# Attention softmax by two sets of scores, one turned, with the maximum added on TensorE, in a step per batch

## The reference, cut to what matters

```python
x = x + L0_xattn(layernorm(x), ctx, ctx, ...)   # rotary embedding on q and k
x = x + L0_ffn(layernorm(x), ...)               # 8 experts, top 2, and a shared one
x = x + L1_xattn(layernorm(x), ctx, mask, ...)  # no rotary; keys masked where mask is 0
x = x + L1_ffn(layernorm(x), ...)               # 16 experts, top 4, and shared ones

# one attention, for each batch and each of 16 heads
q = (query @ Wq.T + bq);  k = (key @ Wk.T + bk);  v = (key @ Wv.T + bv)
scores = einsum('bhsd,bhtd->bhst', q, k) / sqrt(16)      # 128 queries x 128 keys
attn = softmax(scores, axis=-1)
out = einsum('bhst,bhtd->bhsd', attn, v)                 # then @ Wo.T + bo
```

## Time and profile before

| what | value |
|---|---|
| three timed runs | 1117.19, 1118.29, 1121.87 us |
| the profiled execution: its own time | 1119.13 us |
| its span, first to last instruction | 1117.3 us |
| TensorE matmul busy / weight load busy | 952.8 us (85%) / 825.7 us (74%) |
| VectorE / ScalarE / GpSimd busy | 776.6 / 581.0 / 436.6 us |
| mean granted TensorE clock | 0.940 of full |

### The profile page before, as it was taken

How to read it: one execution, slowest core, us unless ns; L and a number is a source line. 1 busy time by engine, 2 the same in 40 slices (tenths; PEclk the granted TensorE clock), 3 DMA queues, 4 the chain that set the end, 5 groups by cost and what they waited for, 6 DMA issues and landing times.

```text
span 1117.3 us, 20415 instructions
## 1 busy us (share of the span) xinstructions
PE 952.8 (85%) x6981; PEld 825.7 (74%) x6981; DVE 776.6 (70%) x1538; ACT 581.0 (52%) x1112; POOL 436.6 (39%) x479
## 2 busy tenths in 40 slices
PE   2798878748987999999837888885989999999995
PEld 2577667536877999999825767665678888888885
DVE  5688787866664777777655687795686666667665
ACT  5375675745234667667546877874622232322221
POOL 1465556240663666666415444334012212212210
PEclk9989999859998999999956899996899999999999
DMA  3300750010325888888540000001000001000002
GB/s 129 110 21 1 189 144 1 1 61 1 128 82 193 237 231 233 227 221 233 119 134 1 20 20 1 1 2 43 15 15 29 28 14 28 17 26 28 14 0 76
DMA packets 44281, 85.81 MB, mean 77 GB/s; under 512 B 4161, under 2 KB 31041, under 8 KB 44097
## 3 DMA queue, kind: packets, MB, share of 16 engines
q0 software_dynamic: 14784, 46.44, 15.1%
q1 hardware_dynamic: 29440, 38.61, 11.9%
HBM read 64.25 MB, written 20.79 MB: 76 GB/s over the span
## 4 chain that ended last, share of the span: by engine, by line
PE 48%; DVE 20%; ACT 11%; issue 9%; DMA 7%; POOL 4%; DVEq 0%; ACTq 0%; POOLq 0%
PE bank L1179 31%; PE bank L1215 8%; DMA w_raw<-in_fw,w_idx 4%; DVE nmax L1034 3%; PE bank L1274 3%; DVE probT_lo L1063 2%; PE bank L1364 2%; DVE prob L1037 2%; POOL sorted_x L375 2%; ACT xn L512 2%; DMA summed<-y_sb,tile_to 2%; ACT probT_hi L654 1%; ACT o_raw L644 1%; PE bank L1343 1%; ACT w_hi L533 1%
## 5 line engine op out<-in xcount | busy, mean ns | idle before, releaser
L1179 PE MATMUL bank<-xT_hi,w_hi 128*128 128x512 f32 x352 | 139.9, 398 | 2.2 <-DVE hid L964 2.2
L581 ACT ACTIVATE act_sb<-bank 128x512 f32<-128x512 f32 x88 | 52.6, 598 | 167.8 <-PE bank L1179 167.7
L1179 PE MATMUL bank<-xT_lo,w_hi 128*128 128x512 f32 x352 | 139.3, 396 | 0.0
L1179 PE MATMUL bank<-xT_hi,w_lo 128*128 128x512 f32 x352 | 139.1, 395 | 0.0
L964 DVE TENSOR_TENSOR hid<-bank,act_sb 128x512 f32<-128x512 f32 x88 | 60.8, 691 | 107.3 <-ACT act_sb L581 107.1
L332 POOL TENSOR_TENSOR w_hi<-w_raw,zero_col 128x768 fp32r<-128x768 f32 (+1 forms) x20 | 31.9, 1595 | 262.9 <-PE bank L1215 236.8
L951 DVE SCALAR_TENSOR_TENSOR xres<-bank,gate,xres 128x256 f32<-128x256 f32 x320 | 132.6, 476 | 0.8 <-PE bank L1215 0.8
L1364 PE MATMUL bank<-ident,prob 128*128 128x128 f32 x512 | 86.2, 298 | 31.9 <-DVE probT_lo L1063 26.0
L1063 DVE TENSOR_TENSOR probT_lo<-bank,probT_hi 128x512 f16<-128x512 f32 x128 | 88.0, 687 | 32.4 <-ACT probT_hi L654 31.8
L1179 PE MATMUL bank<-xsT_hi,w_hi 128*128 128x256 f32 x368 | 106.5, 289 | 2.3 <-DVE xsT_lo L918 1.5
L1215 PE MATMUL bank<-w_hi,hid_hi 128*128 128x256 f32 x352 | 99.5, 283 | 6.2 <-DVE hid_lo L972 6.2
(11 more groups left out here) (199 smaller groups left out, 2763.5 us busy)
## 6 DMA issues: line engine op xcount, KB each, us to landing
w_raw<-in_fw SPq DMA_DIRECT2D x18, 384.0 KB, 3.0
sorted_x<-empty_row SPq DMA_DIRECT2D x2, 2967.0 KB, 21.4
xs<-sorted_x SPq DMA_DIRECT2D x23, 258.0 KB, 3.4
ctx_raw<-in_ctxT SPq DMA_DIRECT2D x8, 512.0 KB, 5.2
aw_raw<-in_aw SPq DMA_DIRECT2D x10, 256.0 KB, 3.8
summed<-empty_row SPq DMA_DIRECT2D x1, 2304.0 KB, 29.6
xres<-in_x SPq DMA_DIRECT2D x4, 512.0 KB, 5.7
xn_all<-summed SPq DMA_DIRECT2D x4, 512.0 KB, 5.9
```

The lines of the kernel that those rows point to most:

```text
L581: nc.scalar.activation(act_sb[:, (ls * J + j) % 2, :], bank[2 * ((ls * J + j) % 2) + 1][:], ACT.Silu).then_inc(f["act"], 1)
L1179: last = nc.tensor.matmul(dst, lh, rh, start=(i == 0), stop=(i == len(pairs) - 1))
```

## The change

Each batch becomes one step, and every engine's program is written out over 16 batches and two steps of tail. Scores are made twice. `scores` makes them queries by keys, only for the maximum: banks 0 to 3, all four row groups, the zeroed copy now being of Q (`q_half`), 128 columns to a product. VectorE's four reductions of a batch write the negated maxima to columns of `low_col`; TensorE turns that tile (`lows_turned`), ScalarE copies it (`low_copy`) to `low_row`. `scores_turned` makes the scores keys by queries in banks 4 to 7 and adds the negated maximum there by products with `pick`, a 0/1 tile that has a one in the row of the head. ScalarE's exponential of a whole bank then gives the probabilities with keys on partitions, so nothing is turned or split: `weighed` multiplies them in float32 by `v_full` (16 columns of V, one of ones, padded to `VW` = 32) with V as the weights, into four 32-partition strips of bank 0. ScalarE copies this, TensorE turns it back (`turned_back`), VectorE normalizes (`output`). The layer 1 mask is a bias of the exponential by key (`mask_col`, one more DMA) and a product in `scores`. Outputs are projected batch by batch.

Layer 0 no longer has the exchanged weights (four weights in place of six): VectorE multiplies one product by cosine and by sine and exchanges partitions in pairs by `stream_shuffle`, GpSimd subtracts. A step makes at most two items of a later block (`build_at`): steps 0 to 2 K0 and K1, Q0 and Q1, V0 and V1 of block 1; steps 3 to 5 and 7 to 9 K0 and V0, K1 and V1, Q0 and Q1 of blocks 2 and 3. GpSimd keeps the rotary subtraction, the context's low part and bias additions. `lowest` in a step waits for all of `scores`.

The diff, cut to its core:

```diff
-VW = 50
-RING, RINGT = 6, 3
+VW = 32
-        W_ORDER = [[2, 3, 0, 1, 4, 5], [1, 2, 0, 3]]
+        W_FROM = [[0, 2, 4, 5], [0, 1, 2, 3]]
+        W_ORDER = [[K_W, Q_W, V_W, O_W], [K_W, V_W, Q_W, O_W]]
@@ sync @@
+                sp.dma_start(mask_col[:], maskrow.rearrange("o (b t) -> (o t) b", t=S),
+                             allow_slow_non_contiguous=True).then_inc(s_in, 16)
@@ scalar @@
+                def attend():
+                    context_high(1)
+                    low_copy(0)
+                    for b in range(B + 2):
+                        if b < B:
+                            exponential(b, 0)
+                            exponential(b, 1)
+                        if 1 <= b <= B:
+                            output_copy(b - 1)
+                        if b < B:
+                            exponential(b, 2)
+                            exponential(b, 3)
+                        if b >= 2:
+                            output_high(b - 2)
...
+                        if b + 1 < B:
+                            low_copy(b + 1)
@@ vector @@
+                    dve.wait_ge(a["rope"], 3 * u + 2)
+                    nc.vector.stream_shuffle(rope_b[:, r], rope_b[:, r], PAIR).then_inc(a["rope"], 1)
...
+                def attend():
+                    lowest(0)
+                    for b in range(B + 2):
+                        if b + 1 < B:
+                            lowest(b + 1)
+                        if b >= 2:
+                            output_low(b - 2)
+                        made = build_at(b)
+                        if made:
+                            made_item(made[0], made[1])
+                        if 1 <= b <= B:
+                            output(b - 1)
+                        if b >= 2:
+                            residual(b - 2)
+                        if made:
+                            made_item(made[0], made[2])
@@ tensor @@
+                def scores(b):
...
+                    for u in range(KT):
+                        for h in range(2):
+                            for r in range(NG):
+                                rows = slice(32 * r, 32 * r + 32)
+                                at_col = 256 * u + S * h
+                                last = nc.tensor.matmul(bank[r][:, at_col:at_col + S], q_half[rows, n % 2, u, h, cols],
+                                                        k_full[rows, n % 2, u, cols], start=(u == 0 and h == 0),
+                                                        stop=(l == 0 and u == KT - 1 and h == 1))
...
+                def scores_turned(b):
+                    n, c = divmod(b, BLK)
+                    if b >= 1:
+                        pe.wait_ge(a["exp"], NG * b)
+                    if b >= 3:
+                        pe.wait_ge(a["xadd"], b - 2)
+                    made = build_at(b - 1) if b else None
+                    for item in made[1:] if made else ():
+                        banks_read(made[0], item)
+                    cols = slice(S * c, S * (c + 1))
+                    for u in range(KT):
+                        for r in range(NG):
+                            rows = slice(32 * r, 32 * r + 32)
+                            nc.tensor.matmul(bank[4 + r][:, 256 * u:256 * u + 256], k_full[rows, n % 2, u, cols],
+                                             q_half[rows, n % 2, u, :, cols], start=(u == 0), stop=False)
+                    pe.wait_ge(a["lowcopy"], b + 1)
+                    for h in range(GRP):
+                        for r in range(NG):
+                            rows = slice(32 * r, 32 * r + 32)
+                            last = nc.tensor.matmul(bank[4 + r][:, S * h:S * (h + 1)], pick[rows, h, :],
+                                                    low_row[rows, b % 2, :], start=False, stop=(h == GRP - 1))
+                    last.then_inc(a["turn"], 1)
...
+                def weighed(b):
+                    n, c = divmod(b, BLK)
+                    pe.wait_ge(a["exp"], NG * (b + 1))
...
+                    if b + 2 < B:
+                        pe.wait_ge(a["max"], NG * (b + 2) + 1)
+                    for pair in range(2):
+                        for u in range(KT):
+                            for q in range(4):
+                                r, j = 2 * pair + q // 2, q % 2
+                                last = nc.tensor.matmul(bank[0][32 * q:32 * q + VW, S * (2 * u + pair):S * (2 * u + pair + 1)],
+                                                        v_full[:, n % 2, c, 8 * u + 2 * r + j, :],
+                                                        prob[:, b % 2, r, S * (2 * u + j):S * (2 * u + j + 1)],
+                                                        start=True, stop=True)
...
+                def attend():
+                    scores(0)
+                    lows_turned(0)
+                    for b in range(B + 2):
+                        made = build_at(b)
+                        if b < B:
+                            scores_turned(b)
+                        if b + 1 < B:
+                            scores(b + 1)
+                        if 1 <= b <= B:
+                            weighed(b - 1)
+                        if b >= 2:
+                            output_turned(b - 2)
+                        if made:
+                            pe.wait_ge(a["exp"], NG * b + 1)
+                            make_item(made[0], made[1])
+                        if 1 <= b <= B:
+                            turned_back(b - 1)
+                        if b >= 2:
+                            projected(b - 2)
+                        if made:
+                            pe.wait_ge(a["exp"], NG * b + 2)
+                            make_item(made[0], made[2])
+                        if b + 1 < B:
+                            lows_turned(b + 1)
```

More of the change, by code:

```diff
@@ L475, in _ @@
-                outputs(NBLK - 1, False)
-                pool.wait_ge(a["xadd"], 2 * NBLK)
+                context_low(a, 1)
+                for b in range(B):
+                    made = build_at(b)
+                    for item in made[1:] if made and l == 0 else ():
+                        if item not in (V0, V1):
+                            rotate(made[0], item)
+                    if b in (2, 5):
+                        context_low(a, 2 + b // 4)
+                pool.wait_ge(a["xadd"], B)
@@ L587, in experts @@
                                              ACT.Copy).then_inc(f["hhi"], 1)
[L589 removed]
+            act.wait_ge(s_set, 2)
             for l in range(2):
@@ new lines, in values @@
+                def values(m, item):
+                    h = (V0, V1).index(item)
+                    if m == 0:
+                        dve.wait_ge(a["vset"], 2)
+                    dve.wait_ge(a["vps"], 2 * m + h + 1)
+                    src = bank[unit_bank(l, m, item)]
+                    for c in range(2):
+                        nc.vector.tensor_tensor(v_full[:, m % 2, 2 * h + c, :, 0:HD],
+                                                src[:, D * c:D * (c + 1)].rearrange("p (h d) -> p h d", h=HEADS),
+                                                bv_row[l][:].rearrange("p (h d) -> p h d", h=HEADS),
+                                                ALU.add).then_inc(a["v"], 1)
@@ L1101, in _ @@
-                    values(0)
+                    for item in (K0, K1):
+                        unit_build(0, item)
+                    weights_low(range(2, NW))
+                    for item in (Q0, Q1):
+                        unit_build(0, item)
+                    for item in (V0, V1):
+                        values(0, item)
                     first_constants()
@@ new lines, in unit, with wt @@
+                def unit(m, item):
+                    u = unit_no(m, item)
+                    w, r = (K_W, Q_W)[item in (Q0, Q1)], u % 2
+                    def wt(part):
+                        return lambda k: part[:, w, k, P * r:P * (r + 1)]
+                    if item in (K0, K1):
+                        pe.wait_ge(a["ctx_lo"], m + 1)
+                        right = (lambda k: ctx_hi[:, k, :], lambda k: ctx_lo[:, k, :])
+                    else:
+                        cols = slice(N * m, N * (m + 1))
+                        right = (lambda k: xT_hi[:, k, cols], lambda k: xT_lo[:, k, cols])
+                    products(bank[unit_bank(l, m, item)][:], (wt(aw_hi), wt(aw_lo)), right).then_inc(a["proj"], 1)
@@ new lines, in values @@
+                def values(m, item):
+                    pe.wait_ge(a["ctx_lo"], m + 1)
+                    h = (V0, V1).index(item)
+                    for c in range(2):
+                        rows = slice(P * (2 * h + c), P * (2 * h + c + 1))
+                        last = products(bank[unit_bank(l, m, item)][:, D * c:D * (c + 1)],
+                                        (lambda k: ctx_hi[:, k, rows], lambda k: ctx_lo[:, k, rows]),
+                                        (lambda k: aw_hi[:, V_W, k, :], lambda k: aw_lo[:, V_W, k, :]))
```

(1 more changed line is left out.)

678 lines of the change are left out of this document (290 added, 388 removed).

## The result

The changed kernel takes 1127.41 us (median of 11 runs, 1123.09 to 1135.96), the kernel before in the same session 1118.81 (11 runs, 1115.91 to 1125.31). The ratio is 1.0081, 95% interval 1.0052 to 1.0111: slower by 0.8%. Forecast were 1099 us and a gain.

The account below looks back on a forecast made before the run. The prediction took VectorE's throughput in the attentions as the bound. Gains of 20.1 us in layer 0 and 8.1 in layer 1, less 9.0 for the clock, made 19.2: from 1119.13 to 1099.9, median 1099, range 1070 to 1165.

Parts of the forecast that it names:

- the clock: TensorE at half clock at the attention entries: one step charged per layer, 4.5 and 4.5 us.
- step 0 of layer 0: First batch step of layer 0's attention, without outputs yet: forecast to take 9.2 us.
- the entry of layer 1: Up to layer 1's first scores: K and V made during layer norm cost nothing; scores at 598.3, not 600.59 us.
- Bound of the kernel before: In the attentions VectorE's throughput binds, with ten reductions or subtractions per batch, one every 0.64 us.
- prices of products: TensorE in a step: four row groups run beside each other, products 0.86, maxima added 0.88, weighed 1.05 us.
- rivals 1 and 2: Row groups pack worse than four: 1183 us, chance 0.23; weighed's four strips run one after another: 1180 us, chance 0.07.
- The step without items: A batch step that makes no unit, one chain through three engines: 8.95 us in layer 0, 9.15 in layer 1.
- The steps with items: Batch steps that also make units: 10.7 to 12.1 us in layer 0, 10.9 or 11.3 in layer 1.
- rival 3: Half clock stays on TensorE over half of the steps, 78 us: 1178 us, chance 0.05.
- The last steps: From step 15 to the last residual of each attention: 12.7 us in layer 0, 12.8 in layer 1.

Follow-up runs that it names:

- e9: e8 with the three transfers that empty the sorted rows and sums cut into twelve parts, each released by one more finished batch: 1078.33 us, ratio 0.9622.
- e3: The changed kernel with the projection in bank 3 in place of bank 6, so the next step's scores_turned need not wait for the residual: 1120.50 us, ratio 0.9988.
- e12: The changed kernel with the three emptying transfers cut into twelve parts, each released by one more finished batch: 1127.49 us, ratio 1.0065.
- e1: The changed kernel with TensorE's idle time in every batch step filled with products that nobody reads: 1123.64 us, ratio 1.0035.
- e4: The changed kernel with both edits, all exponentials ahead of output_copy and the projection in bank 3: 1087.42 us, ratio 0.9710.
- e5: e4 with GpSimd making the low part of the context's second block before the bias additions, in both layers: 1088.38 us, ratio 0.9721.
- e2: The changed kernel with all four exponentials ahead of output_copy on ScalarE: 1094.56 us, ratio 0.9773.
- e7: e5 with VectorE's layer norm ahead of the bias on the first values in layer 1: 1089.05 us, ratio 0.9732.
- e10: e8 with more dummy products behind the last batch and behind each block of the layer norm that follows: 1087.80 us, ratio 0.9710.
- e11: e9 with the dummy products of e10 behind the last batch and the following layer norm: 1088.91 us, ratio 0.9712.
- e6: The changed kernel with the dummy products of e1 only in batch steps that make no unit: 1121.90 us, ratio 1.0010.
- e8: e7 with dummy products behind each layer's first scores and, in layer 1, behind each block of the layer norm: 1077.69 us, ratio 0.9636.

## Why the prediction was wrong, by its own steps

The forecast gain of 19.2 us became a loss of 8.6. Three terms of the sum failed: the clock (9 us charged), step 0 of layer 0 (9.2 us), and the entry of layer 1 (a gain of 2.3 us). That 1127 lies inside the stated range of 1070 to 1165 is luck: its upper part was there for row groups that pack badly, and they don't.

**Bound of the kernel before, prices of products: right.** Four row groups run wholly beside each other (1.15, 1.10 and 1.08 us), so rivals 1 and 2 fell. The Trainium skill (TensorE: Matmul & The Clock Gate, Measured speedup vs the span model) has four row tiles at 3.07 times one, which gave 1125. That this is near 1127 is chance: the trace shows four groups with twice the work of two in 0.02 us more.

**The step without items: right to 0.2 us.** Forecast 8.95 and 9.15, measured 9.16 and 9.37 at full clock. The term is the pair of exponentials behind the copy: 1.06 by the earlier trace rows, 1.26 in the trace.

**The steps with items: right at full clock.** K and V 11.28 (11.4), V alone 10.85 (10.7), two queries 11.93 (12.1); layer 1 11.06 (10.9) and 11.7 (11.3).

**Clock: the step that failed most.** The working charged one half-clock step per layer, at the entries, because a stretch that was busy 7.1 of 10 us kept full clock, and gave half clock inside the stage a chance of 0.05 (rival 3). Steps are busy 6.17 of 9.16 us, and the clock fell in eight places of layer 0 and five of layer 1. Rival 3's mechanism was thus right, its price wrong: a step that meets a stretch of 3.41 us loses 1.6 us (10.8 for 9.16), not 4.9, as only a third of it is at half clock.

What the clock cost in all is an estimate, from steps measured at full clock. Layer 0 adds up to 12.54 + 10.78 + 10.85 + 4 x 11.28 + 2 x 11.92 + 6 x 9.16 + 12.88 = 171.0 us, layer 1 to 7.0 + 10.17 + 5 x 11.06 + 2 x 11.7 + 6 x 9.37 + 12.88 = 165.0 (its step 0 from e9, where the entry is filled; the way from step 15 on from e3). The profile of the changed kernel is 14.5 and 10.6 us above these sums, 1.7 of it waits for instructions, that of e12 11.4 and 6.0. So the clock took some 17 to 23 us inside the attentions, against 9 charged. By the same sums the dummies of e1 cost 3 us in layer 0 and near 11 in layer 1 (174.2 and 175.8), which is why its full clock gave so little. The rest of the miss in the two attentions is the walk: 171.0 for 167.0, 165.0 for 161.8.

**Step 0: mis-sized. The last steps: right.** Step 0 of layer 0 was to take 9.2 and took 12.54. The working followed three engines and said of GpSimd only that it loses work, "which ends no stage now". It still does the low part of the second block, behind four bias additions of 2.34 us, and the diff makes the first step want it: 3.1 us of idle TensorE (e4), 2.8 of them back in e5. With the entry filled the step takes 8.97. The way from step 15 to the last residual, forecast 12.7, takes 12.88 where no half-clock stretch meets it (layer 0 of e3):
```profile
211.91:224.79 12.88, 9.26 (x145) 7.17 (x144) 4.25 (x12) 6.00 (x11) 0.00 (x0) 1.00 0.01 3
```
The 15.8 of the changed kernel met two such stretches (218.6 and 225.4 us).

**Entry of layer 1: wrong in sign.** Making K and V while the layer norm runs, "which costs nothing since TensorE waits for that anyway", held for TensorE and not for VectorE. Its first sum comes 5.89 us after the issue of the rows, against 4.33 before; with the same order it came after 4.37 in e1 and 6.64 in e2, and with the values moved behind it after 4.28 (e7). And GpSimd's additions, which now run beside the layer norm, lengthen two small operations by 1.1 and 0.9 us. 33.75 forecast, 38.00 measured, 36.04 before. The stages of e5 and e7 give back 2.8, and in e5 the way from the first sum to the scores is 29.36, as forecast (29.4).

**What was seen and not used.** The working names the two ready exponentials queued behind `output_copy` and prices them correctly; the forecast follows from that. So it is no reason of the miss, but it is the largest single thing that the change lost: that place costs 32.9 us (e2), some 21 in the chain and the rest in the clock. With it in the other order the same idea is 2.3% faster than the kernel before.

What stays open: 6 us of spread between the profiles in the stretch of unchanged code between the layers (331.9 to 337.9, e10 and e11 aside), of which no run here names the cause, where the half-clock stretches fall, and why e3's half-clock stretches come in layer 1 and not in layer 0.

## What to carry to other kernels

When a change turns an engine bound by throughput into a chain through several engines, walk each in-order queue for work that is ready but stands behind a wait: here moving two instructions on ScalarE took 0.5 to 1.15 us out of each step and, with the clock that came back, was worth 32.9 us. Filling TensorE's gaps inside the steps gave 5.5 by the medians at best (e6), at the entries 11.4 (e8 against e7). Then charge the clock for each step of the new chain and not for the entries alone, and walk the queue of the engine that seems idle too, since it feeds the first step. Dummy products paid where TensorE waited for longer than they last (e8); in e10, where its own work was due behind them, the kernel got 10 us slower.

## What the runs showed of the hardware

- Four row groups of 32 rows, and four column strips of 32, run with no loss against one another: 16 instructions of 256 columns in 1.15 us, 32 of 128 columns in 1.08 to 1.10.
- The granted clock fell to half in steps where no wait of TensorE was longer than 1.23 us, in stretches of 3.41 us or multiples of it (after), and stayed full when nine bf16 products a step filled the waits (e1).
- A VectorE operation on 128x4 elements took 1.22 us in place of 0.16 while GpSimd added 128x1024 elements in SBUF.
- With the DMA engines busy 90% or more, TensorE stood up to 3.28 us inside a run of matmuls with nothing to wait for but its own instructions; this came in five of ten profiles, and in none of three with the same transfers in parts.
- ScalarE took 0.60 us to copy a bank of 128x512, 0.68 for an exponential and 0.695 for an addition, both with a bias column.
- A shuffle of 128x512 float32 took 0.73 us, forecast 0.6.
